# Second attention layer: head turn earlier, filler products, another drain order, and the first layer's small transfers on ScalarE

## The reference

```python
x = x + gate_a0 * recurrent_attention(modulate(layernorm(x)))   # layer 0, scan over 512 tokens, 16 heads of 8
x = x + gate_b0 * moe(modulate(layernorm(x)))                   # layer 0: shared expert + 2 of 8 experts
x = x + gate_a1 * windowed_attention(modulate(layernorm(x)))    # layer 1, "second attention"
x = x + gate_b1 * moe(modulate(layernorm(x)))                   # layer 1: 2 of 8 gated experts
```

## Time and profile before

| | us |
|---|---|
| median of three runs | 1328.71 (1327.28 to 1329.68) |
| profiled execution, its time | 1323.83 |
| profiled execution, its span | 1322.0 |
| mean granted clock of TensorE | 0.914 of full speed |
| PE / DVE / ACT / POOL busy | 1151.1 / 839.1 / 504.6 / 599.5 |

### The profile page before, as it was taken

One profiled execution on the slowest core, in us unless ns is written; L12 is line 12 of the kernel. 1 busy time (PEld: TensorE's weight loads), 2 busy tenths in 40 slices (PEclk: granted clock), 3 DMA queues, 4 the chain that ended last, 5 costly groups with the idle time before them and its releaser, 6 DMA issues.

```text
span 1322.0 us, 24049 instructions
## 1 busy us (share of the span) xinstructions
PE 1151.1 (87%) x8101; PEld 782.1 (59%) x8101; DVE 839.1 (63%) x2229; ACT 504.6 (38%) x1147; POOL 599.5 (45%) x701
## 2 busy tenths in 40 slices
PE   6868769867788888898999999999987799999996
PEld 3445446645358886344454455545534499999993
DVE  4668978787334444425658688686667366666664
ACT  3324434433314442033434444443342145444440
POOL 1556768877525554513143454463135333333330
PEclk9889989898889999878978889888898899999998
DMA  4976787673124522201011120110002231111105
GB/s 135 255 187 158 174 253 170 154 169 82 35 76 121 149 76 63 68 1 45 12 46 39 32 60 25 53 42 19 23 26 52 74 120 45 38 46 37 42 22 199
DMA packets 87313, 113.07 MB, mean 86 GB/s; under 512 B 11224, under 2 KB 68888, under 8 KB 84616
## 3 DMA queue, kind: packets, MB, share of 16 engines
q1 hardware_dynamic: 77720, 91.07, 26.2%
q0 software_dynamic: 8640, 17.84, 4.1%
q10 hardware_dynamic: 832, 2.63, 0.6%
HBM read 81.06 MB, written 32.04 MB: 86 GB/s over the span
## 4 chain that ended last, share of the span: by engine, by line
PE 58%; DVE 13%; issue 9%; DMA 8%; POOL 6%; ACT 4%; SPq 2%; DVEq 1%; another core or an unknown queue 0%; ACTq 0%; POOLq 0%
PE bank L2111 8%; PE bank L2122 8%; PE bank L2221 5%; PE bank L2269 4%; PE bank L2138 3%; PE bank L2233 3%; PE bank L2278 3%; PE bank L2308 3%; DMA region<-vrdram 3%; PE bank L2297 2%; DVE region L933 2%; POOL slots L1289 2%; DMA vrdram<-wgl 1%; DVE bank L931 1%; PE bank L1874 1%
## 5 line engine op out<-in xcount | busy, mean ns | idle before, releaser
L1289 POOL DMA_INDIRECT slots<-pay,slot x128 | 129.9, 1015 | 141.4 <-issue 114.6
L2111 PE MATMUL bank<-rows,wup 128*128 128x128 f32 x1136 | 156.3, 282 | 17.0 <-DVE wup L779 15.3
L2111 PEld LDWEIGHTS bank<-rows,wup 128*128 128x128 f32 x1136 | 142.4, 197 | 21.1 <-DVE rows L767 13.3
L1304 POOL DMA_INDIRECT y<-region,xin x78 | 83.7, 1073 | 154.5 <-ACT region L1683 140.8
L1783 ACT ACTIVATE w0uv<-bank 128x512 f32<-128x512 f32 x192 | 99.1, 603 | 136.3 <-PE bank L2278 105.9
L2122 PE MATMUL bank<-rows,wse 128*128 128x128 f32 x1136 | 141.8, 278 | 1.4 <-DVE wse L784 1.3
L2122 PEld LDWEIGHTS bank<-rows,wse 128*128 128x128 f32 x1136 | 132.5, 192 | 7.2 <-issue 6.1
L1052 DVE TENSOR_REDUCE rows<-bank 128x4 f32<-128x512 f32 x128 | 79.4, 683 | 53.7 <-PE bank L2221 52.2
L1304 POOL DMA_INDIRECT y<-hh,region x64 | 69.7, 1089 | 91.7 <-ACT hh L1683 81.9
L772 DVE SCALAR_TENSOR_TENSOR rows<-bank,bcol,rows 128x128 f32<-128x128 f32 x142 | 43.4, 346 | 91.8 <-ACT rows L1672 91.7
L1874 PE MATMUL bank<-consts 128*128 128x512 f32 x178 | 88.7, 647 | 4.5 <-DVE region L1074 4.5
(11 more groups left out here) (355 smaller groups left out, 2422.2 us busy)
## 6 DMA issues: line engine op xcount, KB each, us to landing
region<-vrdram SPq DMA_DIRECT2D x16, 1024.0 KB
region<-vrdram SPq DMA_DIRECT2D x32, 512.0 KB, 8.0
xin<-slots SPq DMA_DIRECT2D x78, 65.0 KB
region<-slots SPq DMA_DIRECT2D x64, 65.0 KB
wgl<-in_wgl SPq DMA_DIRECT2D x8, 512.0 KB
rows<-y SPq DMA_DIRECT2D x8, 512.0 KB, 4.3
xres<-x SPq DMA_DIRECT2D x12, 256.0 KB
wgl<-in_x SPq DMA_DIRECT2D x8, 256.0 KB
```

Of the source, the lines that this page charges most:

```text
L1289: p.indirect_dma_start(io["slots"], bass.IndirectOffsetOnAxis(ap=slot_of(l, b)[:, k, t:t + 1], axis=0), pay_of(l, b)[:, k, t, :], None).th ...
L1304: p.indirect_dma_start(io["y"], bass.IndirectOffsetOnAxis(ap=xins[par][:, h, k, P + 1:P + 2].bitcast(U32), axis=0), bYs[par][:, h, k, :], ...
L2111: ins = M(bank_up(l, n)[:, tile(j)], wup[:, n % 3, tile(j)], bxT[:, q % 2, tile(k)], start=True, stop=True)
```

## The change

It has four parts.

1. **Layer 0.** `load_second` and `store_second` leave SP and are issued by ACT. The load of the gate row is split off (`load_gate` on ACT), counted on its own semaphore and issued at the end of the step before the one that uses it. `Xs` is loaded behind ACT's `reception(a)`, and the finished rows are stored behind ACT's `shared(c)`.
2. **Second attention, every step.** `turn(b)` moves on PE from behind the second `score_local` to behind the first one, and `norm_local(b)` moves on DVE ahead of `max_local(i, 0)`. One `keep_busy` product is added ahead of `score_local(i, 0)` and one ahead of `score_global(a, 1)`.
3. **Drain.** In the last step DVE does `norm_global(7)` and the first half of `router(6)` ahead of `mix`, and `take_local(7, 0)` ahead of the second half; PE routes batch 6 before the gate. The last batch's residual has a tile of its own (`xf`), loaded ahead of time. In `tail`, `gate` comes before `h2_T` and one `keep_busy` goes; POOL no longer waits for the scatters of batches 6 and 7.
4. **End.** `keep_busy(10, ...)` is added ahead of the last sums.

```diff
                     sp.wait_ge(S["mod_st"], 16)
-                if ok(b):
-                    load_second(b)
                 if ok(a):
...
                     load_rows(a, 0)
-                if ok(c):
-                    store_second(c)
                 if ok(a):
...
             def tail(t):
+                sp.wait_ge(S["c_xh1"], NB * NT)
+                sp.wait_ge(S["c_owg"], (t - 1) * 3 + 2)
+                settled(sp)
+                sp.dma_start(xf, xres_of(t)).then_inc(S["load_k"], 16)
+                sp.dma_start(mrow[:, M_GA, :], io["mods"][1, t, M_GA * P:(M_GA + 1) * P].partition_broadcast(P)).then_inc(S["load_k"], 16)
                 sp.wait_ge(S["c_xh2"], (t - 1) * 4 + 4)
                 sp.dma_start(xres_of(t - 1), X).then_inc(S["st_x1"], 16)
-                sp.wait_ge(S["st_x1"], (t - 1) * 16 + 16)
-                settled(sp)
-                sp.dma_start(X, xres_of(t)).then_inc(S["load_k"], 16)
-                sp.dma_start(mrow[:, M_GA, :], io["mods"][1, t, M_GA * P:(M_GA + 1) * P].partition_broadcast(P)).then_inc(S["load_k"], 16)
                 sp.wait_ge(S["c_h2"], (t - 1) * 2 + 2)
...
                 settled(sp)
-                sp.dma_start(xres_of(t), X).then_inc(S["st_x1"], 16)
+                sp.dma_start(xres_of(t), xf).then_inc(S["st_x1"], 16)
                 sp.wait_ge(S["st_x1"], t * 16 + 16)
...
                 a, b, c, d, f = i + 1, i - 1, i - 2, i - 3, i + 2
+                if ok(b):
+                    norm_local(b)
                 if ok(i):
                     max_local(i, 0)
-                if ok(b):
-                    norm_local(b)
                 if ok(a):
...
                     take_global(i, i % 2)
+                if i == LAST:
+                    norm_global(i, i % 2)
+                    router(1, c, 0.0, 0)
                 if ok(f):
...
                     mix(b, b % 2)
+                if ok(i):
+                    take_local(i, 0)
                 if i == LAST:
-                    router(1, c, 0.0, 0)
                     router(1, c, 0.0, 1)
                     place(1, c)
-                if ok(i):
-                    take_local(i, 0)
                 if ok(c) and i < LAST:
...
                     residual(b)
-                if i == LAST:
-                    norm_global(i, i % 2)
                 if ok(a):
...
             def gated_out(b):
-                p.wait_ge(S["load_b0"], 32 * b + 32)
+                p.wait_ge(S["load_s"], 16 * b + 16)
                 if b:
...
                 p.wait_ge(S["load_k"], 32 * b + 32)
+                if b == LAST:
+                    p.wait_ge(S["c_proj"], b)
                 G_.tensor_tensor(owg[:, :], wo1[:, :], mrow[:, M_GA, :], ALU.mult).then_inc(S["c_owg"], 1)
                 p.wait_ge(S["c_owg"], 3 * b + 2)
-                G_.tensor_tensor(X, X, bc(obg[:, :], NT, 1), ALU.add).then_inc(S["c_owg"], 1)
+                G_.tensor_tensor(X_of(b), X_of(b), bc(obg[:, :], NT, 1), ALU.add).then_inc(S["c_owg"], 1)
...
                     scatter(1, b, 1)
-                    scattered(1, b)
             p.wait_ge(S["prep_v"], MASKS)
...
+            def load_gate(b):
+                if b:
+                    a.wait_ge(S["a_owg"], b)
+                else:
+                    a.wait_ge(S["mod_st"], 16)
+                settled(a)
+                a.dma_start(mrow[:, M_GA, :], io["mods"][0, b, M_GA * P:(M_GA + 1) * P].partition_broadcast(P)).then_inc(S["load_s"], 16)
+
+            def load_second(b):
+                if b >= 2:
+                    a.wait_ge(S["st_x0"], 16 * (b - 1))
+                settled(a)
+                a.dma_start(Xs[b % 2], xsrc[b]).then_inc(S["load_b0"], 16)
+
+            def store_second(c):
+                a.wait_ge(S["b_x"], c + 1)
+                settled(a)
+                a.dma_start(xres[c], Xs[c % 2]).then_inc(S["st_x0"], 16)
+
             def decide(b):
...
                 if ok(b):
+                    load_second(b)
+                if ok(b):
                     scale_heads(b)
...
                     shared(c)
+                    store_second(c)
                 if ok(n):
...
                     routed_again(b)
+                if ok(i):
+                    load_gate(i)
             recurrent_rows(step)
...
                     t_.wait_ge(S["c_gm"], b + 1)
+                if b and t == 1:
+                    t_.wait_ge(S["c_neg"], b * NEG_STEPS)
+                    keep_busy(1, bank[5])
                 for g in range(NHG):
...
                     t_.wait_ge(S["c_xm"], b * HG + HG)
+                    keep_busy(1, bank[6])
                 for t in range(2):
...
                     score_local(i, p, 0)
+                if ok(b):
+                    turn(b)
                 if ok(d):
...
                     score_local(i, p, 1)
-                if ok(b):
-                    turn(b)
                 if ok(d):
...
                 turn(t)
+                gate(t, t % 2)
                 h2_T(t - 1)
-                gate(t, t % 2)
                 route(t - 1)
-                keep_busy(1, bank[7])
                 out(t)
...
             t_.wait_ge(S["m_yb"], BLOCKS)
+            keep_busy(10, bank[BANK_Y])
             for b in range(SUMMED, NB):
...
```

More of the change, by code:

```diff
@@ L244, in out_bank, with X_of @@
             return bank[4] if b < LAST - 1 else bank[5]
+        def X_of(b):
+            return xf if b == LAST else X
         def pay_of(layer, b):
@@ L388, in y_loaded @@
                 return f"load_y{b}", 16
-            name, earlier = (("load_a", 16 * NB), ("load_d", 16 * NB), ("load_s", 16 * NB), ("load_b0", 32 * NB))[b - NB // 2]
+            name, earlier = (("load_a", 16 * NB), ("load_d", 16 * NB), ("load_s", 32 * NB), ("load_b0", 16 * NB))[b - NB // 2]
             return name, earlier + 16
@@ L464, in load_first @@
                     load_x(a)
-            def load_second(b):
-                if b:
-                    sp.wait_ge(S["a_owg"], b)
-                if b >= 2:
-                    sp.wait_ge(S["st_x0"], 16 * (b - 1))
-                settled(sp)
-                sp.dma_start(Xs[b % 2], xsrc[b]).then_inc(S["load_b0"], 16)
-                sp.dma_start(mrow[:, M_GA, :], io["mods"][0, b, M_GA * P:(M_GA + 1) * P].partition_broadcast(P)).then_inc(S["load_b0"], 16)
             def load_gate(c):
@@ L492, in store_reception @@
                 sp.dma_start(vrdram[a % 2, 1], rS).then_inc(S["st_v"], 16)
-            def store_second(c):
-                sp.wait_ge(S["b_x"], c + 1)
-                settled(sp)
-                sp.dma_start(xres[c], Xs[c % 2]).then_inc(S["st_x0"], 16)
             def load_rows(a, n):
@@ L1845, in tail @@
                 mixed_T(t, t % 2)
+                gate_tanh(t)
                 h2_T(t - 1)
-                gate_tanh(t)
                 second_copy(1, t - 1)
@@ L2422, in step @@
                     again_local(i, p, 0)
+                if i == LAST:
+                    route(c)
                 if ok(b):
@@ L2426, in step @@
                     score_global(a, a % 2, 2)
-                if i == LAST:
-                    route(c)
                 if ok(i):
                     attend_local(i, 0)
-                    again_local(i, p, 1)
                 if i == LAST:
                     rank(1, c)
+                if ok(i):
+                    again_local(i, p, 1)
                 if ok(b):
```

13 lines of the change are left out of this document (6 added, 7 removed).

## The result

| | before | changed kernel |
|---|---|---|
| median of the first comparison (us) | 1327.19 | 1325.89 |
| the ten executions of the changed kernel that the ratio uses (us) | | 1298.1 to 1309.0 |
| ratio | 1 | **0.9835 [0.9802, 0.9867]**, repeated 0.9838 [0.9804, 0.9873] |

The ratio is 22 us, or about 1306.8 us beside the 1328.71 on which the prediction stood: inside the range, 8 us above the forecast of 1299. The profile shown is that of an execution of 1301.68 us (span 1299.8; run e1_after_again, which has the changed kernel as it is).

The account below looks back on a forecast made before the run. It took a chain of waits, chiefly GpSimd's for the gate row, to bound the first stage, and TensorE at low clock the second attention. -17 - 6.5 - 5.7 - 0.5 = -29.7 us from 1328.71 gave 1299 us; range 1281 to 1317.

Parts of the forecast that it names:

- Part 1, -17: First layer: moving three transfers from SyncE to ScalarE's own queue saves 17 us; bounds -23.4 and +28.
- Sum 23.4 us. What is late next: `Xs` ... Near enough that I take three quarters: First layer: gate-row waits ahead of owg free 23.4 us; Xs may be late next, so -17 us is taken.
- the rival that I gave 0.07: First layer: ScalarE, held until its own store lands, loads Xs late; +28 instead of -17, about 1344 us; chance 0.07.
- VectorE rarely waits: First layer: freeing the loads of region's two later groups from store_second is booked as nothing, as VectorE rarely waits.
- the two rules that the prediction weighed: First-layer transfers: engines' transfers interleave, so the row lands no earlier; or queues take turns by packet, so it passes the backlog.
- about when SyncE issued it: First layer: ScalarE asks for the gate row about when SyncE had issued it, but no longer behind the backlog.
- Part 2, -6.5: Second attention: moving turn costs +4 us over seven steps at equal clock, the clock gives -10.5; sum -6.5 us.
- I take half: Second attention: of some 75 us at 1.2 GHz within reach, half is recovered: 37 x 0.285 = -10.5 us.
- both answer in full: Rival: first-layer transfers (-23.4) and second-attention clock (-19.8) give all they can; 1283 us; chance 0.13.
- The rival that the gap at `turn`'s old place takes over the fall: Second attention: the clock does not answer, falling in the new gap instead; 1309.5 us; chance 0.20.
- Parts 3 and 4, -6.2: Drain reordering saves 5.7 us; ten products ahead of the last sums save 0.5 us at the end.
- -5.7: Drain: take_local(7, 1) begins 4.5 us earlier and fewer keep_busy at full clock save 1.2 us; bounds -8 and 0.

Follow-up runs that it names:

- e1: The changed kernel once more, with all four parts, against the kernel before: ratio 0.9838, -21.5 us.
- e2: The kernel before with part 1 alone (gate row, Xs load and finished rows' store issued by ScalarE): ratio 0.9954 to before, -6.1 us.
- e6: The kernel before with all of part 1 and a third tile for Xs: ratio 0.9894 to before, -13.7 us.
- e5: The kernel before with only the gate row moved to ScalarE; Xs load and store stay on SyncE: ratio 0.9946 to before, -7.0 us.
- e10: The changed kernel with a third tile for Xs, turn staying at the head: ratio 0.9761 to before, -30.9 us.
- e7: The kernel before with turn and norm_local moved as in part 2, no keep_busy products added: ratio 1.0049 to before, +6.3 us.
- e12: The changed kernel (two tiles for Xs) without the keep_busy product ahead of score_local(i, 0): ratio 0.9945 to before, -7.1 us.
- e8: The kernel before with part 2's two keep_busy products per step, turn and norm_local where they were: ratio 0.9934 to before, -8.5 us.
- e9: The changed kernel with a third tile for Xs, and turn and norm_local back in their old places: ratio 0.9806 to before, -25.1 us.
- e11: The changed kernel (two tiles for Xs) without the keep_busy product ahead of score_global(a, 1): ratio 0.9867 to before, -17.2 us.
- e3: The kernel before with part 2 alone (turn and norm_local moved, two keep_busy products): ratio 0.9967 to before, -4.4 us.
- e4: The kernel before with parts 3 and 4 alone (drain and end): ratio 0.9969 to before, -4.1 us.

## Why the prediction was right, and where it was not

**The direction and the range were right; the forecast was 8 us too low**, and the main term was wrong in size. Some of the agreement is luck: timed alone, the parts sum to half of the forecast (-14.6 of -29.7).

*Part 1, -17, measured -6.1.* The step that failed is "Sum 23.4 us. What is late next: `Xs` ... Near enough that I take three quarters". The six waits for the gate row were added up as if each stood on the path by itself, and the only successor that I priced was `Xs`. The successor was the rival that I gave 0.07, ScalarE held by its own store. I had put its threshold at a landing of 10.7 us and argued against it with the median of 8.0 us; the one in e2's chain took 11.58. That rival's mechanism was right and its price was wrong: it takes some 7.6 us (e2 against e6), not the 45 by which I let the part turn to +28, since ScalarE would have stood there for TensorE most of that time (54.4 us in before, 66.9 in e2). With the third tile the term is -13.7 (interval -18.5 to -9.1), near my price. `Xs` was late as well: in e5 TensorE waited 19.3 us for it. And that "VectorE rarely waits" for the loads of `region` was a wrong reading (24.1 us in 10 waits in before), though the term is small: in e2, with SyncE's order freed, it was still 22.2 us in 7.

*The queue itself.* The waits for the gate row went from 30.6 us to 3.7 (e1), but no run decides between the two rules that the prediction weighed. I had written that the row is asked for "about when SyncE issued it"; in fact ScalarE issued it earlier, by 6 to 10 us in e1's first four batches, and SyncE's issue itself had taken up to 11.19 us where ScalarE's took 0.34. Both shorten the wait without any overtaking, and behind the 2 MB load the row came no faster in its own queue (16.5 us against 16.6). By the Trainium skill, "DMA: Bandwidth & Descriptors", section "Queues, rings and completion order", DMA engines take turns between the queues that have work. The trace neither shows nor refutes it here: the row landed in 5.8 us in the median with a queue to itself and in 10.6 with the store and `Xs` beside it. What would decide is a run in which SyncE issues the row as early as ScalarE did; there is none.

*Part 2, -6.5, measured -4.4 alone (interval -9.0 to 0), and -13 beside the others* (e10's -30.9 less 13.7 and 4.1; some 7 us either way). Alone, turn and products were near their prices: +6.3 against +4, and -8.5 against -10.5. Together in e10 the step "I take half" was too low: by the clocks and lengths of steps 1 to 6, 58 of the 70 us at the low level are gone, nearer to my case *both answer in full* (-15.8 for this part). The account that each edit covers one place at the head of the step, and that the clock needs both, fits e7, e10 and e12, but it is argued and not shown: e8 and e9 kept the full clock in one step without the turn's cover, e11 in two without the second product, and e10 lost it in steps 0, 2 and 6 with both. The rival that the gap at `turn`'s old place takes over the fall came true in part: there lies the second fall in e7 and e12, and the falls in steps 2 and 6 of e10. In steps 3 to 5 of e10 it did not.

*Parts 3 and 4, -6.2, measured -4.1 (interval -6.8 to -1.6).* In e1 the last `turn` came 57.1 us behind the start of step 7, before it was 61.2: -4.1 where I had said 5 to 6. But the second experts began only 0.9 us nearer to the start of step 7. Of the 3.2 us that were lost on the way, the chains of waits say where. Behind the last `turn` both go through VectorE's routing to ScalarE's normalisation (`xh`) and then to SyncE (start and length; e1, then before):

```profile
989.61 1.66 ACT xh L1775 x4
...
993.66 16.37 issue
```
```profile
1014.63 1.66 ACT xh L1764 x4
...
1018.69 14.38 issue
```

`xh` starts 13.9 us behind the last turn, before 13.4. From its end to the code of SyncE that stores the padding it is 18.8 us, before 16.8, and from there to the landing of the first load of the second experts some 0.8 us more than before, with a wait of 2.1 us for a padding store in it. What SyncE did in the long piece no view shows, so the cause of the 2 us stays open. The step that failed is that -5.7 took every microsecond of the last `turn` as one of the kernel, with nothing for what follows it. The last sums ran at full clock from their first product, 10.46 us for 24 records, which is the estimate; the end is 0.6 us shorter.

**What stays open.** I cannot say why the executions of e3 lie 29 us apart, and those of the changed kernel 37; the 35 of before beside them lie 17 us apart, 34 of them within 10. The trace of e3 has steps of 58 us, and in them ScalarE began its fourth exponentials 3.3 us after the last product that they wait for had ended by the record (806.37 + 1.44 = 807.81), with TensorE waiting for them behind the second product:

```profile
811.11 1.08 ACT L1783 ACTIVATE w0uv<-bank 128x512 f32<-128x512 f32 x2 [4.58 <-remote]
```
```profile
806.37 1.44 PE L2282 MATMUL bank<-rows,pick_g 32*128 32x512 f32 x5
807.73 1.12 PE L1874 MATMUL bank<-consts 128*128 128x512 f32 x2
811.76 0.69 PE L2224 MATMUL bank<-rows,wsh 32*128 32x512 f32 x1 [2.90 <-ACT w0uv L1783]
```

The first profile of the changed kernel, an execution of 1335.19 us, has the same four waits (18.3 us) and steps of 58.0 us, and its first experts began at 385.9 us; that of 1301.68 us has none of these waits. No trace of e7 or e8, which have one edit each, shows this wait, and the six runs of e10, which has both, lie within 11 us. The experiments do not tell whether the third tile, the other chip or chance kept it away.

## What to carry to other kernels

A wait that disappears is worth what the next one on its path leaves: before adding up waits, ask for each which wait ends just behind it, and for a store that is moved to another engine, who now waits for its landing on that engine. A further tile for the data is often the cheaper half of such a move. When the clock falls behind short waits, look at every wait in the stretch before moving work between them: work that is moved to cover one may leave the next open, and then costs time. And when the executions of one kernel lie as far apart as its gain is large, give their range beside the gain.

## What the runs showed of the hardware

- A row of 64 KB landed in 2.9/5.8/10.1 us (shortest, median, longest) with a second hardware queue to itself (e5), and in 3.5/10.6/16.6 us with two transfers of 256 KB a batch in that queue beside it (e6). A store of 256 KB landed in 2.3/3.1/5.4 us from SyncE's queue (e5) and in 2.3/11.1/17.7 us from ScalarE's (e6).
- Behind a load of 2 MB the issue of a 64 KB row took 11.19 us on SyncE (before, the same queue) and 0.34 us on ScalarE (e1, the other queue); the row was there 16.6 and 16.5 us after the start of its issue.
- The same move can have opposite signs by what stands beside it: `turn` +6.3 us without the two products, -5.8 us with them (the latter with overlapping intervals).
- The clock fell behind waits of 0.69, 0.89 and 0.92 us, and behind one of 0.36 us in one step of e10 but not in the three steps ahead of it, whose products and wait were the same there.
- The same kernel differed by 33 us between one chip and two others. The stretch from the first experts to the attention took 174.1 to 175.8 us on the first (e1 to e4) and 146.8 to 151.7 us on the others (e5, e8 to e12); in before, TensorE waited there 15.3 us for VectorE's copies of weights (`wup`), in e1 16.0 us, and in e5, e8 and e10 not at all.
